# Expert results of a gated mixture-of-experts: plain scatter to six tables instead of adding into two

## The reference

```
xf = layernorm(x)                                  # 1024 x 256
scores = sigmoid(xf @ w_router)                    # 32 experts
topk_idx = 6 best experts of the 4 best groups, by scores + corr_bias
combine[t, e] = scores[t, e] for the 6 chosen, else 0
eo[e, t] = (silu(xf @ gate_w[e]) * (xf @ up_w[e])) @ down_w[e]     # inner width M = 176
routed[t] = sum over e of combine[t, e] * eo[e, t]
out = x + tanh(g_ffn) * (routed + shared_expert(xf))
```

## Time and profile before

| what | value |
|---|---|
| median of three runs | 329.17 us |
| profiled execution, its span | 334.7 us |
| PE busy | 274.3 us (82%) |
| DVE, ACT, POOL busy | 126.2, 99.2, 166.9 us |
| bytes moved | 57.20 MB, mean 171 GB/s |
| mean granted TensorE clock | 0.935 |

### The profile page before, as it was taken

One profiled execution on the slowest core, in us unless ns is written; L12 is line 12 of the kernel. 1 busy time (PEld: TensorE's weight loads), 2 busy tenths in 40 slices (PEclk: granted clock), 3 DMA queues, 4 the chain that ended last, 5 costly groups with the idle time before them and its releaser, 6 DMA issues.

```text
span 334.7 us, 6384 instructions
## 1 busy us (share of the span) xinstructions
PE 274.3 (82%) x1107; PEld 160.8 (48%) x1108; DVE 126.2 (38%) x627; ACT 99.2 (30%) x267; POOL 166.9 (50%) x145
## 2 busy tenths in 40 slices
PE   4673879999205997998999999999999999999700
PEld 3531445555002654655565655555566555665300
DVE  4568689433100331332333333333333333333214
ACT  3452411111001332333333333333333333333200
POOL 3334777777700153344555555555555555465620
PEclk9999999999655998999999999999999999999955
DMA  5899999999974589995666566666666666664577
GB/s 157 266 319 366 352 343 314 314 230 254 240 154 114 156 211 259 229 249 91 100 99 99 98 100 89 113 100 89 96 109 96 94 100 100 100 99 71 59 170 240
DMA packets 58557, 57.20 MB, mean 171 GB/s; under 512 B 6544, under 2 KB 56432, under 8 KB 58544
## 3 DMA queue, kind: packets, MB, share of 16 engines
q1 hardware_dynamic: 43520, 36.51, 39.6%
q0 software_dynamic: 13136, 18.78, 34.0%
q10 hardware_dynamic: 1888, 1.78, 2.5%
HBM read 32.35 MB, written 24.70 MB: 170 GB/s over the span
## 4 chain that ended last, share of the span: by engine, by line
PE 53%; SPq 24%; DMA 15%; issue 4%; DVE 1%; ACT 1%; DVEq 0%; POOLq 0%; ACTq 0%
PE pG L578 23%; PE pY L594 11%; PE pY L593 8%; PE pX L649 7%; DMA sum_dram<-xnT,idx 6%; SPq L225 5%; SPq L222 5%; DMA rows_dram<-pad_rows 4%; SPq L227 4%; SPq L255 4%; DMA rows<-rows_dram 3%; SPq L256 3%; PE pH L584 2%; PE pH L585 2%; DMA xnT<-sum_dram 1%
## 5 line engine op out<-in xcount | busy, mean ns | idle before, releaser
L384 POOL DMA_INDIRECT sum_dram<-xnT,idx x71 | 110.0, 1549 | 119.1 <-ACT xnT L486 94.9
L578 PE MATMUL pG<-wgu,rows 128*128 x284 | 99.9, 476 | 2.0 <-ACT rows L476 1.5
L855 DVE COPY hT<-pH 128x128 f32<-128x128 f32 x87 | 25.3, 291 | 119.7 <-PE pH L585 117.9
L578 PEld LDWEIGHTS pG<-wgu,rows 128*128 128x128 f32 x284 | 49.9, 196 | 19.8 <-issue 5.4
L365 POOL DMA_INDIRECT rows_dram<-rows,row_i x48 | 47.3, 986 | 21.3 <-issue 14.2
L486 ACT ACTIVATE xnT<-pY,wt 128x256 f32<-128x256 f32 x71 | 33.7, 474 | 73.9 <-PE pY L594 41.8
L462 ACT ACTIVATE sg<-pG 128x176 f32<-128x176 f32 x87 | 27.6, 317 | 90.9 <-PE pG L578 90.9
L594 PE MATMUL pY<-wd,hT 48*128 x142 | 49.4, 428 | 0.0
L649 PE MATMUL pX<-ident,rows 128*128 128x128 f32 x142 | 31.7, 306 | 21.0 <-DMA rows<-rows_dram 21.0
L593 PE MATMUL pY<-wd,hT 128*128 x142 | 42.6, 382 | 0.0
L649 PEld LDWEIGHTS pX<-ident,rows 128*128 128x128 f32 x142 | 14.8, 144 | 44.8 <-issue 40.1
(11 more groups left out here) (145 smaller groups left out, 168.7 us busy)
## 6 DMA issues: line engine op xcount, KB each, us to landing
rows<-rows_dram SPq DMA_DIRECT2D x71, 144.5 KB, 2.2
wgu<-in_L_ffn_gate_w_dram SPq DMA_DIRECT2D x8, 704.0 KB, 7.6
wgu<-in_L_ffn_up_w_dram SPq DMA_DIRECT2D x8, 704.0 KB, 9.1
wd<-in_L_ffn_down_w_dram SPq DMA_DIRECT2D x8, 512.0 KB, 8.4
rows_dram<-pad_rows SPq DMA_DIRECT2D x21, 144.5 KB, 12.7
sum_dram<-pad_rows POOLq DMA_DIRECT2D x2, 1152.0 KB, 10.9
rows_dram<-pad_rows ACTq DMA_DIRECT2D x12, 144.5 KB, 8.4
wd<-in_L_ffn_down_w_dram SPq DMA_DIRECT2D x8, 192.0 KB, 7.4
```

Of the source, the lines that this page charges most:

```text
L384: pool.indirect_dma_start(sums_dram[s % SUMS][:, :], bass.IndirectOffsetOnAxis(ap=idx[:, s:s + 1], axis=0), y[:, s, :], None, compute_op=A ...
L578: ins = nc.tensor.matmul(pG[par][:, 0:2 * M], left(k), w(k), start=(k == 0), stop=(k == K - 1))
```

## The change

The row in `rows_dram` grows to `H + 2 * E` = 320 numbers = 1280 bytes: beside each weight it now carries, for each expert, the row of a new DRAM table `picks_dram` to which that expert's result for this token goes. Token t's n-th choice has row n * T + t; pad rows go to spare rows at the table's end. DVE works the numbers out with a scan over `chosen`. The results are written by an indirect transfer that copies and does not accumulate, so POOL no longer waits for earlier ones, and the two tables are not cleared. At the end all six parts of 1024 rows are read (into the memory of the gate and up weights) and added one after the other.

```
-    ROW = H + E + 1
+    ROW = H + 2 * E
...
-    SUMS = 2
+    SPARE = T * (TOPK + 1)
...
-        sums_dram = [nc.dram_tensor(f"sum{i}_dram", [T + P, H], F32, kind="Internal").ap() for i in range(SUMS)]
+        picks_dram = nc.dram_tensor("picks_dram", [SPARE + E * P, H], F32, kind="Internal").ap()
...
-        work = sb("work", [P, 4, H])
+        work = wd1_all[:, E - 4:E, :]
...
+        picks = wgu[:, :, :, :].rearrange("p e k m -> p (e k m)")[:, 0:TOPK * J * H].rearrange(
+            "p (r j c) -> p r j c", r=TOPK, j=J)
...
-            sp.wait_ge(s_taken, last * RING + (RING + REST))
+            sp.wait_ge(s_gu, last * RING + (RING + REST + UNITS))
             sp.sem_inc(s_passed, 1)
-            sp.wait_ge(s_xTc, last * RING + (RING + REST))
-            sp.sem_inc(s_passed, 1)
-            for i, into in ends:
-                for s in range(i, RING, SUMS):
-                    sp.wait_ge(s_add[s], (last + (2 if s < REST else 1)) * 16)
-                    sp.sem_inc(s_passed, 1)
-                for b in range(B):
-                    js = slice(b * HALVES, (b + 1) * HALVES)
-                    sp.dma_start(into[:, js, :],
-                                 sums_dram[i][0:T, :].rearrange("(j p) c -> p j c", p=P)[:, js, :]).then_inc(s_sums[i][b], 16)
+            for s in range(RING):
+                sp.wait_ge(s_add[s], (last + (2 if s < REST else 1)) * 16)
+                sp.sem_inc(s_passed, 1)
+            for r in range(TOPK):
+                sp.dma_start(picks[:, r, :, :],
+                             picks_dram[(r + 1) * T:(r + 2) * T, :].rearrange("(j p) c -> p j c", p=P)).then_inc(s_picks[r], 16)
...
-            for i in range(SUMS):
-                pool.dma_start(sums_dram[i].rearrange("(j p) c -> p j c", p=P),
-                               pad_rows[:, 0:H].unsqueeze(1).to_broadcast([P, J + 1, H])).then_inc(s_clear, 16)
...
-                if not first or s >= SUMS:
-
-                    pool.wait_ge(s_add[(s - SUMS) % RING], 16 * i + (16 if s >= SUMS else 0))
-
                 pool.wait_ge(s_yc, t + (J + 1))
                 pool.sem_inc(s_go, 1)
-                pool.indirect_dma_start(sums_dram[s % SUMS][:, :], bass.IndirectOffsetOnAxis(ap=idx[:, s:s + 1], axis=0),
-                                        y[:, s, :], None, compute_op=ALU.add).then_inc(s_add[s], 16)
+                pool.indirect_dma_start(picks_dram[:, :], bass.IndirectOffsetOnAxis(ap=idx[:, s:s + 1], axis=0),
+                                        y[:, s, :], None).then_inc(s_add[s], 16)
...
-                V.scalar_tensor_tensor(comb[:, g, :], scores[:, g, :], tg[:, 1:2], chosen[:, g, :],
-                                       op0=ALU.mult, op1=ALU.mult)
+                link(V.scalar_tensor_tensor(comb[:, g, :], scores[:, g, :], tg[:, 1:2], chosen[:, g, :],
+                                            op0=ALU.mult, op1=ALU.mult))
+                link(V.tensor_tensor_scan(nth[:, g, :].rearrange("p j e -> p (j e)"), chosen[:, g, :].rearrange("p j e -> p (j e)"),
+                                          zero_e[:, 0:1].to_broadcast([P, len(js) * E]), 0.0, ALU.add, ALU.add))
+                V.scalar_tensor_tensor(rows[:, g, H + E:ROW].bitcast(I32), nth[:, g, :], float(T),
+                                       pick_base[:, g].unsqueeze(2).to_broadcast([P, len(js), E]), op0=ALU.mult, op1=ALU.add)
...
-                V.tensor_copy(idx[:, s:s + 1], xg[:, s, H + E:ROW].bitcast(I32)).then_inc(s_taken, 1)
+                V.tensor_copy(idx[:, s:s + 1], xg[:, s, bass.ds(e + (H + E), 1)].bitcast(I32)).then_inc(s_taken, 1)
...
-            for i, routed in ends:
-                for b in range(B):
-                    js = slice(b * HALVES, (b + 1) * HALVES)
-                    dve.wait_ge(s_sums[i][b], 16)
-                    ins = V.tensor_tensor(xs[:, js, :], xs[:, js, :], routed[:, js, :], ALU.add)
-                    if i == LAST_SUM:
-                        ins.then_inc(s_fin, 1)
-                if i != LAST_SUM:
-                    link(ins)
+            for r in range(TOPK - 1):
+                dve.wait_ge(s_picks[r], 16)
+                link(V.tensor_tensor(xs[:, :, :], xs[:, :, :], picks[:, r, :, :], ALU.add))
+            dve.wait_ge(s_picks[TOPK - 1], 16)
+            for b in range(B):
+                js = slice(b * HALVES, (b + 1) * HALVES)
+                V.tensor_tensor(xs[:, js, :], xs[:, js, :], picks[:, TOPK - 1, js, :], ALU.add).then_inc(s_fin, 1)
```

More of the change, by code:

```diff
@@ L74, in gated_xattn_moe @@
         rows_dram = nc.dram_tensor("rows_dram", [IDLE + P, ROW], F32, kind="Internal").ap()
-        sums_dram = [nc.dram_tensor(f"sum{i}_dram", [T + P, H], F32, kind="Internal").ap() for i in range(SUMS)]
+        picks_dram = nc.dram_tensor("picks_dram", [SPARE + E * P, H], F32, kind="Internal").ap()
         wgu = sb("wgu", [P, E, K, 2 * M])
         wd0 = sb("wd0", [P, E, H])
-        wd1 = sb("wd1", [M2, E, H])
+        wd1_all = sb("wd1_all", [P, E, H])
+        wd1 = wd1_all[0:M2, :, :]
         sgu = sb("sgu", [P, SH, K, 2 * M])
@@ L117, in gated_xattn_moe @@
         scores = sb("scores", [P, J, E])
+        nth = scores
         gkey = sb("gkey", [P, J, GROUPS + 8 - TOPK_GROUPS])
@@ L123, in gated_xattn_moe @@
         chosen = sb("chosen", [P, J, E])
+        pick_base = sb("pick_base", [P, J])
+        pick_base_i = sb("pick_base_i", [P, J], I32)
         chosen_b = sb("chosen_b", [P, J, E], BF16)
@@ L182, in gated_xattn_moe @@
         s_shw, s_expw = sem("s_shw"), [sem("s_expw0"), sem("s_expw1")]
-        s_const, s_clear = sem("s_const"), sem("s_clear")
+        s_const = sem("s_const")
         s_dve = sem("s_dve")
@@ L203, in gated_xattn_moe @@
         s_add = [sem(f"s_add{i}") for i in range(RING)]
-        s_sums = [[sem(f"s_sum{i}_{b}") for b in range(B)] for i in range(SUMS)]
+        s_picks = [sem(f"s_pick{r}") for r in range(TOPK)]
         s_fin, s_out = sem("s_fin"), sem("s_out")
@@ L339, in _ @@
             pool.tensor_copy(part_f[:, :], part_i[:, :])
-            pool.iota(rows[:, :, H + E:ROW].bitcast(I32).rearrange("p j o -> p (j o)"), pattern=[[P, J]], base=0,
-                      channel_multiplier=1).then_inc(s_const, 1)
+            for js in PLACED:
+                ins = pool.iota(pick_base_i[:, js.start:js.stop], pattern=[[P - TOPK * T, len(js)]],
+                                base=js.start * P, channel_multiplier=1)
+            chain(ins)
+            pool.tensor_copy(pick_base[:, :], pick_base_i[:, :]).then_inc(s_const, 1)
             chain(pool.memset(pad_rows[:, :], 0.0))
-            chain(pool.iota(pad_rows[:, H + E:ROW].bitcast(I32), pattern=[[0, 1]], base=T, channel_multiplier=1))
+            chain(pool.iota(pad_rows[:, H + E:ROW].bitcast(I32), pattern=[[P, E]], base=SPARE, channel_multiplier=1))
             pool.sem_inc(s_const, 1)
@@ L370, in _, with turn @@
             pool.wait_ge(s_tiles, 1)
-            pool.wait_ge(s_clear, 16 * SUMS)
-            def turn(i, s, first=False):
+            def turn(i, s):
                 t = i * RING + s
-                if not first or s >= SUMS:
-                    pool.wait_ge(s_add[(s - SUMS) % RING], 16 * i + (16 if s >= SUMS else 0))
                 pool.wait_ge(s_yc, t + (J + 1))
                 pool.sem_inc(s_go, 1)
-                pool.indirect_dma_start(sums_dram[s % SUMS][:, :], bass.IndirectOffsetOnAxis(ap=idx[:, s:s + 1], axis=0),
-                                        y[:, s, :], None, compute_op=ALU.add).then_inc(s_add[s], 16)
+                pool.indirect_dma_start(picks_dram[:, :], bass.IndirectOffsetOnAxis(ap=idx[:, s:s + 1], axis=0),
+                                        y[:, s, :], None).then_inc(s_add[s], 16)
             for s in range(RING):
-                turn(0, s, first=True)
+                turn(0, s)
             last = load_last(pool)
```

## The result

The changed kernel takes 335.41 us, the median of four runs (334.52 to 336.95); the kernel before takes 329.18 beside it (328.31 to 332.16). The ratio is 1.016, with a 95% interval of 1.011 to 1.022. The forecast was 329.7, in a range of 323.5 to 337.0: the time lies in the range, 5.7 us above the forecast. The change makes the kernel slower, clear of the noise, by 1 to 2%. The profiled span went the other way, from 334.7 to 332.6 us. Both halves of that have to be explained.

The account below looks back on a forecast made before the run. PE bounds most of the span, with three losses: a full DMA queue before the loop, 7.1 us of loop stalls, an idle end. Front -6.5, loop -5.5, end +12.5 sum to +0.5: span 335.2, median 329.7 us, range 323.5 to 337.0.

Parts of the forecast that it names:

- Front, -6.5: Before the routed loop: DMA queue stops deciding, POOL's scatter pace does; first load at 94.9 instead of 101.38, 6.5 us won.
- the bound of -6.9: Before the routed loop: the most the change was said to win there, 6.9 us; the other bound was 0.
- 60 ns, by the output's rate: Front: lowest price of a 1280-byte row on one engine, at the output's write rate; a gain of 13.0 us.
- wide rows cost by the byte: Rival, front: 1280-byte rows priced by bytes cost 5.6 us, so the front gains only 1.3; time 334.9; chance 0.18.
- The first tile loads say the same of reads: Tile loads of 1156-byte rows: 120 GB/s at share 0.50, 240 at full share, so reads are dear like the writes.
- DVE's extra work: Routing work before the first scatter: 0.65 us more, later steps 0.65 and 0.85; cost 0 if the front ends after 88.
- Loop, -5.5: Tiles 3 to 15: 7.1 us of stalls, 5.5 won without add waits and with cheaper plain writes, 1.6 left to weight loads.
- the 7.1 are the weights' doing: Loop's lower bound: the 7.1 us of stalls come from the last weight loads, so only 1 us is won.
- the rival on the weights: Rival, loop: weight loads hold the loop, which then gains 1.5 us; time 333.7; chance 0.08.
- End, +12.5: After the loop: 6.29 MB of tables read instead of 2.10, at 355 GB/s, adds covered; 12.5 us lost, bounds +10.6 and +20.6.
- tables at the routed rows' rate: Rival, end: tables read at 240 GB/s, so 6.03 MB take 25.1 us instead of 17.0; time 337.8; chance 0.14.
- its opposite: End: faster table reads; by the skill's fit six reads take 16.4 us instead of 21.0 and the time would be 325.1.

## Why the prediction was right, and where not

*Which step failed.* "All is counted against the span of 334.7. The median is 329.17, 5.5 less; I carry the difference over one to one." In every run with a span the time is 1.8 to 1.9 us more than the span, never less. A profiled span above the median says that this execution was longer than the timed ones, or came from a slower chip, and its stalls may then not all be there to be won. Against its own profile the forecast was +0.5 us and -2.1 came; against the timed runs +6.2 came. Of the 7.4 us between the profiled execution and the median, the loop and the end, priced by the means of the table, account for 3.7 (210.3 - 207.7 and 18.6 - 17.6, rounded). The rest, 3.7 us, is not shown anywhere. The timed runs of 329.2 have a span of 327.3; if loop and end took their means there (207.7 and 17.6), the first gate matmul would start at 102.0, not 105.7, and the front's gain would be 4 instead of 7.6; but no profile of the kernel before at 329 us was taken, and this is worked out, not shown.

*Front, -6.5.* The first load came 7.7 us earlier, beyond the bound of -6.9. The mechanism was right: the DMA queue no longer decides, POOL's pace does. The last scatter was issued at 91.04 (91.55 forecast) and landed in 2.5 us (3.2). The share of the two edits was wrong: I gave 6.9 us of DMA time to the clears and took the rows as not dearer. The runs show the row alone to win all of it, and the clears nothing on top. The bound "60 ns, by the output's rate" was right: 331 GB/s at a share of 0.96 is 59 ns for 1280 bytes. The rival "wide rows cost by the byte" is refuted where the front is bound by DMA. The reading "The first tile loads say the same of reads" was wrong: with wide rows the quiet loop's share did not fall (0.63 for 0.62), so the odd length is not what makes the reads cost 77 ns. The rule of the Trainium skill (DMA: Bandwidth & Descriptors, How a descriptor splits into AXI transactions) made the widening free, by the prediction's estimate. The reads of the quiet loop agree with that; the writes into full engines don't, where 1280-byte rows took 59 to 62 ns and 1156-byte rows 80 to 90. Whether alignment is the reason there, the rows of 1284 bytes don't decide.

*DVE's extra work* cost nothing, as said.

*Loop, -5.5.* 5.3 us less between tiles 3 and 15 and 6.0 over the whole loop against that profile; 4 against the mean of all. It was mostly the adds: taking them away alone is worth about 3 us by the means. The weight loads can be behind no more than the 1.2 to 2.7 us of stalls that stay. The bound of -1 for "the 7.1 are the weights' doing" and the gain of 1.5 in the rival on the weights are two numbers for one case.

*End, +12.5.* It became 11.5 against that profile and 12.6 against the mean. Reads began at 4.1 us behind PE's last matmul (4.5 forecast), ran at 348 GB/s (355), and the last adds started 20.5 us after the first issue (21.0). DVE's five big adds took 2.29 us each and were covered. The rival "tables at the routed rows' rate" is refuted, and so is its opposite: the fit of the Trainium skill (DMA: Bandwidth & Descriptors, Anatomy of one DMA) gives an estimate of 16.4 us for the six reads, and 20.5 were measured. The page made that fit for transfers that GpSimd issues; these are SyncE's.

*The sum.* With front -7.7, loop -4.2 and end +12.6 the change is worth +0.7 us where the front is bound by DMA. The kernel with clears put back took 335.79 beside 333.88, +1.9, and the lower end of its interval (1.002 to 1.011) is +0.7. Where something else holds the front the sum is +8.4, and +10.7 was measured (364.34 beside 353.64). On that chip the wide rows with adding were 1.4 us slower than the kernel before, so part of the missing 2 us may be the row's; and the changed kernel was 9.3 us behind them, near the +8.4. On the chip of the main comparison +6.2 was measured. Not even the front's gain of 4, as worked out above, accounts for it: that makes +4.4. So 1.8 us of the main result, and whether the front differs there, stay open.

*The better version.* The wide rows alone, with adding kept, take the front's gain and leave the end as it was: 325.8 us, 2.6% under the kernel before. Where something else holds the front, they win nothing and were 1% slower (1.011, 1.005 to 1.017).

## What to carry to other kernels

A profile whose span is longer than the timed runs shows stalls that those runs may not have: take a second one, on the chip of the runs, before crediting a change with them. Split a change into its edits and price each alone; here the one that paid was the side effect, a wider table row, and only on a chip where the DMA queue held the front. Giving up adding won about 3 us in the loop, but the four further tables then have to be read at the end, where nothing covers them, for 12 us.

## What was not expected of the hardware

In writes from the SBUF to DRAM with the DMA engines full, rows of 1156 bytes took 80 to 90 ns of an engine each and rows of 1280 bytes 59 to 62; as the queue ran empty, rows of 1156 bytes took 55 to 64. In the reads of the quiet loop the two widths cost the same. The same kernel took 329, 334 and 353 us on different chips; in the profiles of its variants on the slowest two, ACT, DVE and PE stood still before the loop for up to 20 us at a time, while POOL and the DMA engines went on.
